# An expert stage written out by slot, with its weights streamed into a ring

## The reference: what is computed

```python
x = x + xattn(layernorm(x), ctx, ctx, mask, ...)      # 16 heads, DK = 8
# ffn, on layernorm(x) once more:
idx    = argmax(softmax(xt @ Wr + br)); gates = max(softmax(...))
xn     = (xt - mu) * rsqrt(var + 1e-5) * ln_g + ln_b
h      = relu(xn @ W1[idx] + b1[idx])                 # W1: 8 x 128 x 512
y      = (h @ W2[idx] + b2[idx]) * gates              # W2: 8 x 512 x 128
x      = x + y
```

## Time and profile before

| | us |
|---|---|
| runs: median (lowest to highest) | 470.75 (468.31 to 471.48) |
| span of the profiled execution | 445.3 |
| median of the runs less this span | 25.45 |
| TensorE busy | 335.5 (75%) |
| VectorE busy | 302.3 (68%) |
| GpSimd busy | 207.4 (47%) |
| ScalarE busy | 202.6 (46%) |

### The profile page before, as it was taken

How to read it: one execution, slowest core, us unless ns; L and a number is a source line. 1 busy time by engine, 2 the same in 40 slices (tenths; PEclk the granted TensorE clock), 3 DMA queues, 4 the chain that set the end, 5 groups by cost and what they waited for, 6 DMA issues and landing times.

```text
span 445.3 us, 12096 instructions
## 1 busy us (share of the span) xinstructions
PE 335.5 (75%) x2988; PEld 243.7 (55%) x2989; DVE 302.3 (68%) x1120; ACT 202.6 (46%) x588; POOL 207.4 (47%) x261
## 2 busy tenths in 40 slices
PE   0578879879889889898967886406888888888870
PEld 0356647658668668676745665303555655555550
DVE  3268999888988988988999895651454545444440
ACT  1158564644554554545565553001545454544540
POOL 5314354354354354354364523313576666666540
PEclk9999996685785775758699785555999999999996
DMA  5921121111111121111121100002222221122110
GB/s 141 381 70 51 33 52 40 35 55 30 30 59 30 30 59 30 30 53 36 35 45 35 32 25 24 26 0 48 55 53 69 59 60 51 59 65 59 50 31 0
DMA packets 35770, 23.64 MB, mean 53 GB/s; under 512 B 11599, under 2 KB 32724, under 8 KB 35744
## 3 DMA queue, kind: packets, MB, share of 16 engines
q1 hardware_dynamic: 29872, 14.99, 12.0%
q0 software_dynamic: 4272, 7.69, 5.9%
q10 hardware_dynamic: 1600, 0.65, 0.6%
HBM read 16.55 MB, written 7.22 MB: 53 GB/s over the span
## 4 chain that ended last, share of the span: by engine, by line
DVE 30%; issue 29%; PE 17%; POOL 7%; DMA 6%; ACT 3%; DVEq 3%; ACTq 1%; POOLq 1%; SPq 0%
PE ps L776 7%; DVE mx L535 6%; PE ps L784 6%; DMA G<-rows_dram,gi 4%; ACT xg L447 3%; DVE lsub L514 2%; DVE xt L501 2%; POOL rs L336 2%; DVE st L569 2%; DVE row L503 1%; DVE Pr L539 1%; PE ps L792 1%; DVE oh L522 1%; DVE rsum L546 1%; DVE st L489 1%
## 5 line engine op out<-in xcount | busy, mean ns | idle before, releaser
L336 POOL TENSOR_TENSOR rs<-ve,half 128x2 f32<-128x2 f32 x32 | 23.1, 723 | 107.3 <-DVE ve L589 103.9
L419 ACT ACTIVATE Pr<-Pr,rowany 128x1024 f32<-128x1024 f32 x32 | 36.7, 1148 | 65.1 <-DVE Pr L539 65.1
L644 DVE COPY hs<-ps 128x512 f32<-128x512 f32 x39 | 27.0, 692 | 52.3 <-PE ps L776 52.3
L368 POOL DMA_INDIRECT out<-ot,si x39 | 39.5, 1013 | 44.1 <-DVE gi L639 20.5
L776 PE MATMUL ps<-W,xg 128*128 x78 | 45.5, 666 | 17.1 <-ACT xg L447 17.1
L692 PE MATMUL ps<-ident,Pr 128*128 128x128 f32 x256 | 54.1, 350 | 2.0 <-ACT Pr L419 1.7
L784 PEld LDWEIGHTS ps<-W,hT 128*128 128x128 f32 x312 | 38.6, 192 | 25.4 <-issue 25.3
L455 ACT ACTIVATE hT<-ps,b1c 128x128 f32<-128x128 f32 x156 | 44.6, 369 | 16.2 <-PE ps L798 10.3
L402 ACT ACTIVATE PT<-ps 128x512 f32<-128x512 f32 x64 | 38.2, 598 | 26.2 <-PE ps L692 25.7
L692 PEld LDWEIGHTS ps<-ident,Pr 128*128 128x128 f32 x256 | 39.0, 180 | 19.5 <-issue 14.9
L361 POOL DMA_INDIRECT G<-rows_dram,gi x39 | 39.9, 1023 | 18.7 <-issue 11.0
(11 more groups left out here) (119 smaller groups left out, 679.0 us busy)
## 6 DMA issues: line engine op xcount, KB each, us to landing
W<-in_w SPq DMA_DIRECT2D x8, 512.0 KB, 8.7
rows_dram<-row SPq DMA_DIRECT2D x32, 128.0 KB
X<-in_x SPq DMA_DIRECT2D x32, 64.0 KB, 1.9
C<-in_ctxT SPq DMA_DIRECT2D x32, 64.0 KB
Cv<-in_ctxT SPq DMA_DIRECT2D x32, 64.0 KB, 2.0
ENT<-table_dram SPq DMA_DIRECT2D x39, 1.0 KB
G<-rows_dram,gi POOLq DMA_INDIRECT x39, 2.8
out<-ot,si POOLq DMA_INDIRECT x39, 2.3
```

What stands on the lines that cost most here:

```text
L368: g.indirect_dma_start(out=out, out_offset=bass.IndirectOffsetOnAxis(ap=si[:, q, :], axis=0), in_=ot[:, q, :], in_offset=None, bounds_chec ...
L419: a.activation(Pr[:, q, :], Pr[:, q, :], ACT.Exp, scale=rowany[:, 0:1]).then_inc(s_p, 1)
```

## The change

1. The host packs for each expert one block of 128 partitions x 1156 float32: W1, W2, b1 and b2, 592 KB. The arrays of all experts in SBUF and their loads at the start are gone.
2. The blocks go into a ring `WR` of NW = 4. SyncE loads one block for each slot, also where two slots have the same expert, 39 in all (23.1 MB). The load of slot s waits until `yb` of slot s-4 is done. It stands on SyncE between the entry loads of s and of s+1.
3. Up has W1 stationary in four blocks of 128 x 128 and `xg` moving, so h comes out transposed. The copy `hs` and the four transposes are gone. The relu is split: ScalarE does two blocks, VectorE two.
4. The stage is written out, 39 rounds on each engine; only SyncE still reads the slot table. GpSimd reads the token numbers from `ENT` directly; the rings `G` and `ot` have 6 buffers, and a gather is issued up to four slots ahead.
5. TensorE's round is: transpose of s+1, up of s, down of s-1.

```diff
-            for e in range(0, E, 2):
-                sp.dma_start(W1[:, e:e + 2, :], w1[e:e + 2].rearrange("e d f -> d e f")).then_inc(s_w[3], 16)
-                sp.dma_start(W2[:, e:e + 2, :, :], w2[e:e + 2]...).then_inc(s_w[3], 16)
...
+            for s in range(SLOTS):                                        # SyncE
+                q, w = s % R, s % NW
+                wait(sp, e_in[q], 16 * (s // R))
+                wait(sp, w_in[w], 16 * (s // NW))
+                first = sp.value_load(slot[0:1, 1, s:s + 1], min_val=0, max_val=ROWS - P)
+                sp.dma_start(ENT[:, s:s + 1, :], table[bass.ds(first, P), :]...).then_inc(e_in[q], 16)
+                wait(sp, b_y, s - NW + 1)
+                sp.dma_start(WR[:, w:w + 1, :], wpk[bass.ds((first >> TB) & (E - 1), 1)]...).then_inc(w_in[w], 16)
...
+            for s in range(-4, SLOTS + 1):                                # GpSimd
+                if s + 4 < SLOTS:
+                    t = s + 4
+                    pool.wait_ge(e_in[q], 16 * (t // R + 1))
+                    wait(pool, b_o, t - R + 1)
+                    g.indirect_dma_start(out=G[:, q, :], ..., in_=rows, ap=ENT[:, t, 0:1], ...).then_inc(g_in[q], 16)
+                if s >= 1:
+                    t = s - 1
+                    pool.wait_ge(b_o, t + 1)
+                    g.indirect_dma_start(out=out, ap=ENT[:, t, 0:1], ..., in_=ot[:, q, :], ...).then_inc(o_out[q], 16)
...
+                    for c in range(2, FC):                                # VectorE
+                        v.tensor_scalar(hT[:, s % 2, P * c:P * c + P], h_ps(s, c), b1_of(s, c), 0.0,
+                                        ALU.add, ALU.max).then_inc(b_rd, 1)
...
+            for s in range(-1, SLOTS + 1):                                # TensorE
+                if s + 1 < SLOTS:
+                    t = s + 1
+                    pe.wait_ge(g_in[t % R], 16 * (t // R + 1))
+                    wait(pe, b_xg, t - 1)
+                    nc.tensor.transpose(ps[:, 4 + t % 2, 0:P], G[:, t % R, D:2 * D], ident[:]).then_inc(b_tx, 1)
+                if 0 <= s < SLOTS:
+                    pe.wait_ge(w_in[s % NW], 16 * (s // NW + 1))
+                    pe.wait_ge(b_xg, s + 1)
+                    for c in range(FC):
+                        last = mm(h_ps(s, c), w1_of(s, c), xg[:, s % 2, :], start=True, stop=True)
+                    last.then_inc(b_up, 1)
+                if s >= 1:
+                    t = s - 1
+                    for c in range(FC):
+                        ...                                               # waits b_ra or b_rd
+                        last = mm(ps[:, 6 + t % 2, 0:D], hT[:, t % 2, P * c:P * c + P], w2_of(t, c), ...)
+                    last.then_inc(b_dn, 1)
```

More of the change, by code:

```diff
@@ L175, in build @@
         psS = ps[:, 0:4, 0:256]
-        s_w = [sem(f"w_in_{n}") for n in ("proj", "small", "mask", "moe")]
+        s_w = [sem(f"w_in_{n}") for n in ("proj", "small", "mask")]
         s_const = sem("consts")
@@ L260, in _ @@
                 sp.wait_ge(e_out[q], 16 * (NP // 2))
[L262 to L269, removed]
+            for s in range(SLOTS):
[3 more added lines that the diff above has]
+                first = sp.value_load(slot[0:1, 1, s:s + 1], min_val=0, max_val=ROWS - P)
+                sp.dma_start(ENT[:, s:s + 1, :], table[bass.ds(first, P), :].rearrange("t (o d) -> t o d", o=1)).then_inc(e_in[q], 16)
+                wait(sp, b_y, s - NW + 1)
+                sp.dma_start(WR[:, w:w + 1, :], wpk[bass.ds((first >> TB) & (E - 1), 1)].rearrange("o p n -> p o n")).then_inc(w_in[w], 16)
             for q in range(R):
@@ L631, in _ @@
             dve.wait_ge(s_slot, 1)
[L632 to L641, removed]
-                    dve.wait_ge(b_up, s + 1)
[L643 to L656, removed]
@@ L658, in _ @@
-            steps(dve, bstep, B0 - 1, BM, B1, R)
+            for s in range(SLOTS + 1):
+                if s < SLOTS:
+                    dve.wait_ge(b_up, s + 1)
+                    wait(dve, b_dn, s - 1)
+                    for c in range(2, FC):
[3 more added lines that the diff above has]
+                    t = s - 1
+                    q = t % R
+                    wait(dve, o_out[q], 16 * (t // R))
+                    dve.wait_ge(b_dn, t + 1)
+                    v.tensor_tensor(out=yb[:, t % 2, :], in0=ps[:, 6 + t % 2, 0:D], in1=b2_of(t), op=ALU.add).then_inc(b_y, 1)
+                    dve.wait_ge(b_y, t + 1)
+                    v.scalar_tensor_tensor(out=ot[:, q, :], in0=yb[:, t % 2, :], scalar=ENT[:, t, 1:2].bitcast(F32),
+                                           in1=G[:, q, 0:D], op0=ALU.mult, op1=ALU.add).then_inc(b_o, 1)
@@ L786, in bstep @@
                                   start=(c == 0), stop=(c == FC - 1))
                     last.then_inc(b_dn, 1)
[L788 to L796, removed]
-                    for c in range(FC):
-                        last = nc.tensor.transpose(ps[:, 2 + q % 2, P * c:P * c + P], hs[:, q % 2, P * c:P * c + P], ident[:])
-                    last.then_inc(b_th, 1)
```

117 lines of the change are left out of this document (51 added, 66 removed).

## The result

| | before | after |
|---|---|---|
| median of 4 runs each, same set, us | 469.53 (466.35 to 471.48) | 495.41 (491.74 to 498.82) |
| ratio | | 1.057 (95%: 1.049 to 1.065) |
| profiled execution, span, us | 445.3 | 492.4 |

The forecast was 473.6 and its range ended at 489, so the result lies outside.

A forecast was written before the change was run, and what follows sets the result against it. Entries behind weights behind y bound the expert stage: (8.47 + 2.2) / 3 = 3.56 us a slot against 3.26. Stage +9.6 and start -6.7 on 445.3 gave 448.2; plus 25.45, 473.6 us; range 456 to 489.

The forecast's parts named there:

- The ring: Expert stage: entries queue behind weights, which wait for y four slots back; three slots per turn, 3.56 us a slot.
- the sum of the turn: Expert stage: waits and landings of 8.47 us plus a TensorE round of 2.2, divided over three slots.
- The round: TensorE in the expert stage: transpose 0.2, up 0.95 and down 1.05, together 2.2 us a slot.
- The gather: GpSimd's gather in the expert stage: 2.84 us to landing plus 0.54 for meeting other slots' weights.
- Start of the weights to entries landed: SyncE's queue in the expert stage: entries land 3.4 us after the weight transfer starts, held behind 592 KB.
- The clock: Rival, chance 0.08: waits slow TensorE's clock in the expert stage; round 4.4 us, slot 4.29, time 503 us.
- The step from span to time: Whole kernel: timed medians lie 25.45 us above the profiled span, added to 448.2 to give 473.6.
- The start: Start of the kernel: without the early weight loads, the first softmax maximum and attention stage come 6.7 us earlier.
- Register reads at nothing: TensorE, ScalarE and VectorE: removing register loads gains nothing, since they ran ahead of the waits.
- Straight-line code at nothing: Expert stage: written-out code in place of the loop costs nothing; the trace shows no fetch stalls in straight-line parts.
- Free entries: Rival, chance 0.24: entries not held by weights, gather meets nothing; turn 7.29 us, slot 3.16, time 459.5 us.
- GpSimd's pace: Rival listed second, chance 0.06: nothing binds but GpSimd's transfers in the expert stage; slot 2.64 us, time 442 us.

The follow-up runs named there:

- e1: The changed kernel with five weight buffers in place of four: 457.14 us (one run), 3.52 us a slot.
- e2: The changed kernel with eight weight buffers in place of four: 445.37 us, ratio 0.957 to the kernel before, 3.23 us a slot.
- e3: The changed kernel, four weight buffers kept, with entry loads issued four slots ahead of the weight loads: 440.93 us, ratio 0.945 to the kernel before.
- e13: The changed kernel, unaltered, timed again in another set: 494.41 us beside a before of 453.7, ratio 1.089.
- e4: The changed kernel with four buffers filled once and only 16 of 1156 weight columns loaded per slot: 461.85 us (one run), 3.84 us a slot.
- e5: The kernel before, unchanged, profiled a second time: 470.9 us, span 469.1, 3.77 us a slot.
- e7: The kernel before with its W1, W2, b1 and b2 loads spread over the first eight attention steps: 461.97 us, ratio 0.984 to before.
- e10: The kernel before with weight loads moved into the first eight attention steps; its intended loop write-out did not happen: 444.46 us, ratio 0.984 to before.
- e18: The kernel before with the expert's number worked out from the loop counter on TensorE, ScalarE and VectorE, loop kept: 446.6 us, ratio 0.984 to before.
- e12: The changed kernel with entries four slots ahead, eight weight buffers and only 16 of 1156 weight columns loaded per slot: 425.02 us (one run).
- e6: The changed kernel with 20 unused identity matmuls in TensorE's long wait ahead of every third transpose: 490.2 us (one run), 4.53 us a slot.

## Why the prediction was wrong

- **The ring: right.** Entries behind weights behind y, three slots a turn: shown by the trace, by e1, which lengthens it, and by e2 and e3, each of which opens it in another way.
- **The failed step is the sum of the turn.** Forecast 10.67 with the round, measured 13.45 in the turn shown. Three terms of it were too small:
  - *The round:* 2.2 forecast, 0.47 + 1.78 + 1.68 = 3.93 measured, +1.73. It runs at a granted clock of 0.51; the forecast reckoned with 1.00 throughout.
  - *The gather:* 2.84 + 0.54 = 3.38 forecast, 4.03 measured, +0.65 (mean of nine on the chain 3.84; in e13, 4.51).
  - *Start of the weights to entries landed:* 3.4 forecast, 1.16 + 2.78 = 3.94 measured, +0.54 (mean of nine 1.16 + 3.09 = 4.25). The forecast let 592 KB drain in 1.56 at the start's 379 GB/s. From 329 to 332 us the engines carried 148, 351 and 195 GB/s, 694 KB in three us, so this block took longer. That the bytes hold the entries shows in e4, where they land in 1.80.

  The small terms are 0.14 shorter together (SyncE and `yb` 0.61 against 0.54, GpSimd's wake 0.79 against 0.87, gather to TensorE 0.05 against 0.13, down to `yb` 0.10 against 0.15): 10.67 + 1.73 + 0.65 + 0.54 - 0.14 = 13.45.
- **The clock was a rival with 0.08.** It gave 503 with a round of 4.4. The rows for it were at hand (0.50 after 290 us); against it the prediction put TensorE's share of busy time, a mean, and overlooked that the wait itself, 3 to 4 us by its own count and 5.6 to 6.6 in the trace, is one idle stretch. The rival's mechanism was there, but with one of three rounds slow in a turn, as it had it, the sum came to 12.87, and the longer transfers make up the rest.
- **The sum by place**, span 492.4 against 448.2 forecast: from the `yb` of slot 5 to that of slot 38 it takes 148.5 instead of 116.2, +32.3; slot table to the `yb` of slot 5 +3.8; the slot table itself +7.7 (297.60; in e1 to e3 and in the same kernel's second trace, e13, it stood at 291.2 to 293.4, so most of this belongs to the execution, and the forecast started from an early 296.6: the other traces with the loads at the start have 299 to 305); the end +0.4.
- **The step from span to time: wrong.** The 25.45 was no constant around the execution, which is 1.7. The execution shown of before was a quick one: 3.23 us a slot where its timed runs must have had about 3.77, as e5 has at the same time. This error (-23.7) hid about half of the other (+44.2): that the time lay only 22 us above the forecast is luck. In the set with a before of 453.7 the loss is 8.9%.
- **The start: right** in mechanism and about in size, 5.9 for 6.7; e7 and e10 put it at 7 to 8 us in the time.
- **Register reads at nothing: wrong** for the kernel before, 0.14 us a slot in e18; the prediction had them run ahead of the waits, and its own trace has the same 6.0 and 5.7 us of idle time on ScalarE and VectorE. In the changed kernel's turn they have no term, so this did not move the forecast. Straight-line code at nothing: open, no run has the kernel before without its loop.
- Free entries, GpSimd's pace: neither came in this kernel. e3 reaches 441 us, the second rival's number, by another way (3.16 us a slot and not 2.64); e12, without the bytes, reaches GpSimd's pace with 2.61.

The Trainium skill ("TensorE: Matmul & The Clock Gate", section on loop structure) has a wait for a DMA between matmuls cool the array; the trace agrees, with 1.78 against 0.89 for eight matmuls at a granted clock of 0.51 against 1.00.

## What to carry to other kernels

When a prefetch ring is shared between a large transfer and a small one that starts a chain of further transfers, issue the small one ahead by its own count; behind the large one's wait, its latency, the gather's and the compute's all add up once a turn. Work out the turn as a sum of landings under load, and divide it by the blocks less one before trusting "four deep". And check that the profiled execution is like the timed ones: time less span is known from one pair, and the 25 us of this case were another execution, not overhead: the step is 1.7. Look in the profile, too, whether an edit did what it was meant to do: with the same number of instructions and the same loop branches nothing has been written out.

## What the runs showed of the hardware

- A 1 KB load behind a 578 KB one in the same queue lands in 3.09 us in the mean, alone in 1.73 (1.80 where the large one is cut to 8 KB); the gather in 3.84 to 4.51 beside the streaming and 3.02 without its bytes.
- In the changed kernel the round after a wait of 5.66 us ran at half the speed of the next; in e6 seven rounds after 1.0 to 2.3 us did not, one after 1.84 us did in part.
- One unchanged program took 451 to 454 us in some sets of runs and 465 to 473 in others, on the same chip too, steady within a set. Its cause isn't settled.
- Working out the expert's number from the loop counter in place of reading it from the slot table on three engines gained 7 us of 454; 6.0 us of ScalarE's and 5.7 us of VectorE's idle time went with the reads.
